# Projection stage of a decoder kernel: four feature steps of a head group issued together, kv sums last, and the last block's queries moved to the last body

## What is computed

```python
qkv = layernorm(x) @ w_qkv                      # 512 -> 3*512
q, k, v = split; 16 heads of 32
q_proj = elu1(einsum('bhnd,hdf->bhnf', q, proj_matrix))   # 128 features a head
k_proj = elu1(einsum('bhnd,hdf->bhnf', k, proj_matrix))
kv    = einsum('bhnf,bhnd->bhfd', k_proj, v)
k_sum = k_proj.sum(axis=2)
# elu1(x) = x + 1 for x > 0, else exp(x)
```

## Time and profile before

| | us |
|---|---|
| median of 3 runs (lowest, highest) | 2795.80 (2794.68, 2798.59) |
| time of the profiled execution | 2796.93 |
| its span, first to last instruction | 2795.2 |
| projection stage within the span | about 0 to 455 |
| PE busy, DVE busy, ACT busy, POOL busy over the span | 2638.4, 1361.0, 858.0, 299.1 |

### The profile page before, as it was taken

One profiled execution on the slowest core, in us unless ns is written; L12 is line 12 of the kernel. 1 busy time (PEld: TensorE's weight loads), 2 busy tenths in 40 slices (PEclk: granted clock), 3 DMA queues, 4 the chain that ended last, 5 costly groups with the idle time before them and its releaser, 6 DMA issues. The chain is left out here.

```text
span 2795.2 us, 34765 instructions
## 1 busy us (share of the span) xinstructions
PE 2638.4 (94%) x12656; PEld 1945.0 (70%) x12680; DVE 1361.0 (49%) x2100; ACT 858.0 (31%) x1364; POOL 299.1 (11%) x228
## 2 busy tenths in 40 slices
PE   7999997899896999799969999999998999999999
PEld 6777774556564554555458888888886888888887
DVE  4544434777765554655463344343335434334433
ACT  3555456455532332133221221111112121112111
POOL 1444343111110111111100000000000000000000
PEclk9999995999997999799989999999999999999999
DMA  6646434554613111212140000000113100000001
GB/s 193 170 98 148 107 87 113 158 156 115 166 75 110 61 54 45 92 61 91 46 155 23 23 23 32 36 23 23 45 45 136 42 26 23 23 23 23 23 23 60
DMA packets 61396, 207.62 MB, mean 74 GB/s; under 512 B 8592, under 2 KB 10384, under 8 KB 50192
## 3 DMA queue, kind: packets, MB, share of 16 engines
q1 hardware_dynamic: 61008, 205.59, 24.4%
q0 software_dynamic: 288, 0.69, 0.1%
HBM read 123.05 MB, written 58.72 MB: 65 GB/s over the span
## 5 line engine op out<-in xcount | busy, mean ns | idle before, releaser
L1876 PE MATMUL ex_pg<-ex_x,ex_w 128*128 128x512 f32 x3840 | 885.5, 390 | 3.3 <-DVE ex_lt L1759 3.3
L1876 PEld LDWEIGHTS ex_pg<-ex_x,ex_w 128*128 128x128 f32 x3840 | 723.3, 188 | 153.7 <-issue 3.5
L1891 PE MATMUL ex_pd<-ex_w,ex_ht 128*128 128x512 f32 x1920 | 446.6, 389 | 0.0
L1825 DVE TENSOR_TENSOR ex_h<-ex_s_g,ex_pg 128x512 f32<-128x512 f32 x160 | 110.1, 688 | 648.6 <-PE ex_pg L1876 647.7
L1891 PEld LDWEIGHTS ex_pd<-ex_w,ex_ht 128*128 128x128 f32 x1920 | 360.5, 188 | 74.7
L1732 ACT ACTIVATE ex_s_g<-ex_pg 128x512 f32<-128x512 f32 x160 | 95.8, 599 | 748.7 <-PE ex_pg L1876 748.6
L1797 DVE SCALAR_TENSOR_TENSOR ex_acc<-ex_pd,ex_share,ex_acc 128x512 f32<-128x512 f32 x320 | 234.4, 748 | 90.3 <-PE ex_pd L1891 84.9
L546 PE MATMUL pr_pj<-pr_xt,pr_w 128*128 128x512 f32 x768 | 194.5, 402 | 4.3 <-DVE pr_xt L443 4.2
L359 POOL TENSOR_TENSOR pr_ks_sum<-pr_ks_sum,pr_kp 128x512 f32<-128x512 f32 x128 | 164.5, 1286 | 228.2 <-DVE pr_kp L490 226.4
L490 DVE SCALAR_TENSOR_TENSOR pr_kp<-pr_pk,pr_kp 128x512 f32<-128x512 f32 x128 | 88.6, 692 | 179.5 <-ACT pr_kp L407 179.1
L546 PEld LDWEIGHTS pr_pj<-pr_xt,pr_w 128*128 128x128 f32 x768 | 142.1, 192 | 33.5 <-issue 2.2
(11 more groups left out here) (175 smaller groups left out, 2856.1 us busy)
## 6 DMA issues: line engine op xcount, KB each, us to landing
stage<-in_units SPq DMA_DIRECT2D x21, 1536.0 KB, 6.6
pr_k<-pr_kq SPq DMA_DIRECT2D x192, 128.0 KB, 2.5
li_q<-q_scratch SPq DMA_DIRECT2D x21, 1024.0 KB, 12.2
q_scratch<-pr_kq SPq DMA_DIRECT2D x128, 128.0 KB, 2.4
x_scratch<-cr_x SPq DMA_DIRECT2D x16, 1024.0 KB, 4.8
pr_x<-in_x SPq DMA_DIRECT2D x8, 1024.0 KB, 6.4
li_x<-in_x SPq DMA_DIRECT2D x8, 1024.0 KB, 5.2
x_scratch<-li_x SPq DMA_DIRECT2D x8, 1024.0 KB, 3.9
```

Of the source, the lines that this page charges most:

```text
L1825: nc.vector.tensor_tensor(h[:, f], s_g[:, f], pg[2 * f + 1][:], ALU.mult).then_inc(h_set, 1)
L1876: mm = nc.tensor.matmul(pg[2 * f + which][:], w[:, slot, sp_, col:col + P], x3[:, m, k, c * TB:(c + 1) * TB], start=(n == 0), stop=(n == 3 ...
L1891: mm = nc.tensor.matmul(pd[t][:], ht[:, s % 2, sp_, f, t * P:(t + 1) * P], w[:, slot, m, WD + f * D:WD + (f + 1) * D], start=(n == 0), sto ...
```

## The change

- PE's loop in a body is no longer by step but by head group g: the four feature steps of the group one behind the other, then a quarter of the body's units, then the four kv sums of this same group. LAG is gone.
- ACT and DVE follow: four steps of exponentials (DVE: four additions), then the reads of all jobs that ended in the group. The statistics of x stand at the end of group 1; the four `norm` stand in group 2, behind the additions and ahead of the reads.
- `kp` has 6 slots for 5, `pk` 4 banks for 3; the kv sums of both batches share one bank (they had one each), and batch 1's first sum waits until DVE has copied batch 0's.
- The four Q jobs of block 7 go from body 6 to body 7; body 6 is left with 8 jobs, body 7 has these 4. Their waits and DMAs move with them.
- SP issues both halves of k and then loads x, where x stood between the halves.

```diff
-    LAG = 2
-    KP_SLOTS, KP_BANKS, BANKS = 5, 3, 3
+    LAST = NBLK - 1
+    KP_SLOTS, KP_BANKS, BANKS = 6, 4, 3
@@ body_jobs
+        if m <= LAST + 1:
+            jobs += [(m if m < LAST else LAST, "Q", g) for g in range(G)] if m != LAST else []
         if m < NBLK:
-            jobs += [(m, "Q", g) for g in range(G)]
@@ plan
-        last = STEPS - 1
-        for s in range(STEPS):
-            part = units[len(units) * s // last:len(units) * (s + 1) // last] if s < last else []
+        for g in range(G):
+            part = units[len(units) * g // G:len(units) * (g + 1) // G]
@@ PSUM
-        p_kv = [... psum_tensor(f"pr_p_kv{b}", [P, 512], F32)) for b in range(NB)]
+        p_kv = ctx.enter_context(nc.psum_tensor("pr_p_kv", [P, 512], F32))
@@ sync
-                        sp.wait_ge(kp_full, STEPS * (m - 1) + (part + 1) * STEPS // PARTS)
+                        sp.wait_ge(kp_full, STEPS * (m - 1) + TT * (2 * part + 2))
...
-                    for part in range(PARTS):
+                    for part in range(PARTS if m < LAST else 0):
                         queries_out(m, part)
                     keys_out(m, 0)
+                    keys_out(m, 1)
...
                         load_x(m + 2)
-                    keys_out(m, 1)
+                for part in range(PARTS):
+                    queries_out(LAST, part)
@@ gpsimd
-                        if n == 6 and i + 2 < NBLK:
+                        if n == 2 * TT - 1 and i + 2 < NBLK:
                             reciprocal_std(i + 2)
@@ scalar
                         if kind == "Q" and m:
-                            act.wait_ge(k3_in[n // 2], 16 * K3_DMAS * m)
-                        if kind == "K":
+                            act.wait_ge(k3_in[n // 2], 16 * K3_DMAS * k_before_q(m))
+                        if kind == "K" and m < LAST:
                             act.wait_ge(q_out[n // 2], 16 * Q_DMAS * (m + 1))
+                        elif kind == "K":
+                            act.wait_ge(k3_in[n // 2], 16 * K3_DMAS * m)
...
-                    for n in range(STEPS):
-                        if i >= 0:
+                    for g in range(G):
+                        for n in range(TT * g, TT * g + TT) if i >= 0 else ():
...
-                        for key in ends(i, n):
+                        for key in ends(i, g):
@@ vector
+                    if i == KV_BODY:
+                        take_kv(0)
+                    for g in range(G):
+                        for n in range(TT * g, TT * g + TT) if i >= 0 else ():
...
+                        if g == 2 and i + 2 < NBLK:
+                            for t in range(TT):
+                                norm(i + 2, t)
+                        for key in ends(i, g):
...
-                        if i == KV_BODY and n == LAG:
-                            take_kv(0)
-                        if i + 2 < NBLK:
-                            if 3 <= n <= 6:
-                                tile_stats(i + 2, n - 3)
-                            if n == 6:
-                                variance(i + 2)
-                            if 8 <= n <= 9:
-                                norm(i + 2, 2 * n - 16)
-                                norm(i + 2, 2 * n - 15)
+                        if g == 1 and i + 2 < NBLK:
+                            for t in range(TT):
+                                tile_stats(i + 2, t)
+                            variance(i + 2)
@@ tensor
+                    if first and i:
+                        pe.wait_ge(kv_taken, i // BLK)
...
-                    for n in range(STEPS):
-                        if i >= 0:
-                            features(i, n)
-                        for key, lo, hi in PLANS[i][n]:
+                    for g in range(G):
+                        for t in range(TT if i >= 0 else 0):
+                            features(i, TT * g + t)
+                        for key, lo, hi in PLANS[i][g]:
                             piece(key, lo, hi)
-                        if i >= 0 and STEPS * i + n >= LAG:
-                            kv(STEPS * i + n - LAG)
-                for step in range(STEPS * NBLK - LAG, STEPS * NBLK):
-                    kv(step)
+                        for t in range(TT if i >= 0 else 0):
+                            kv(i, TT * g + t)
```

More of the change, by code:

```diff
@@ L222, in project, with ends @@
     PLANS = {i: plan(i) for i in range(-1, NBLK)}
-    def ends(i, n):
-        return [key for key, _, hi in PLANS[i][n] if hi == length(key)]
+    def ends(i, g):
+        return [key for key, _, hi in PLANS[i][g] if hi == length(key)]
     JOBS = [(0, "T", t) for t in range(TT)]
@@ L263, in project @@
         pk = [ctx.enter_context(nc.psum_tensor(f"pr_pk{n}", [P, 512], F32)) for n in range(KP_BANKS)]
-        p_kv = [ctx.enter_context(nc.psum_tensor(f"pr_p_kv{b}", [P, 512], F32)) for b in range(NB)]
+        p_kv = ctx.enter_context(nc.psum_tensor("pr_p_kv", [P, 512], F32))
         w_in, x_in = [sem(f"w_in{n}") for n in range(3)], sem("x_in")
@@ L278, in bank_of @@
             return pj[POS[key] % BANKS]
+        k_before_q = lambda m: m if m < LAST else m + 1
         def slot(n):
@@ L381, in take @@
                         if kind == "Q" and m:
+                            act.wait_ge(k3_in[n // 2], 16 * K3_DMAS * k_before_q(m))
+                        if kind == "K" and m < LAST:
+                            act.wait_ge(q_out[n // 2], 16 * Q_DMAS * (m + 1))
+                        elif kind == "K":
                             act.wait_ge(k3_in[n // 2], 16 * K3_DMAS * m)
-                        if kind == "K":
-                            act.wait_ge(q_out[n // 2], 16 * Q_DMAS * (m + 1))
                         nc.scalar.copy(kq[:, HI, n], bank_of(key)[:]).then_inc(act_read, 1)
@@ L452, in take_kv @@
                         dve.wait_ge(filled, POS[(b - 1, "KV")] + 1)
-                    nc.vector.tensor_copy(kv_sum[:], p_kv[b][:]).then_inc(kv_taken, 1)
+                    nc.vector.tensor_copy(kv_sum[:], p_kv[:]).then_inc(kv_taken, 1)
                 def kv_out(b):
@@ L560, in ready @@
                     else:
-                        if kind == "Q" and key[2] == 0:
+                        if kind == ("Q" if m < LAST else "K") and key[2] == 0:
                             pe.wait_ge(dve_read, DVE_AT[(m, "T", TT - 1)])
@@ L579, in features, with kv @@
                     mm.then_inc(kp_full, 1)
-                def kv(step):
-                    i, n = step // STEPS, step % STEPS
+                def kv(i, n):
                     g, t = n // TT, n % TT
+                    step = STEPS * i + n
                     pe.wait_ge(kp_set, step + 1)
@@ L587, in kv @@
                     first, last = i % BLK == 0 and n == 0, i % BLK == BLK - 1 and t == TT - 1
+                    if first and i:
+                        pe.wait_ge(kv_taken, i // BLK)
                     for j in range(HG):
                         h = g * HG + j
-                        mm = nc.tensor.matmul(p_kv[i // BLK][j * HD:(j + 1) * HD, g * F:(g + 1) * F],
+                        mm = nc.tensor.matmul(p_kv[j * HD:(j + 1) * HD, g * F:(g + 1) * F],
                                               v[:, i % 2, t, h * HD:(h + 1) * HD], slot(step)[:, j * F:(j + 1) * F],
```

## The result

| | before | after |
|---|---|---|
| median of 6 runs (us) | 2797.65 | 2777.94 |
| lowest to highest | 2794.68 to 2799.49 | 2765.42 to 2784.84 |
| span of the profiled execution | 2795.2 | 2777.9 |

The ratio is 0.9924, interval 0.9901 to 0.9948: 0.8% faster. The forecast was 2782.5, range 2769 to 2799. The runs spread: over 20 later runs the kernel before went from 2787.66 to 2804.76, so a difference of a few us rests on the profiles and not on the medians.

What follows compares the result with a forecast made beforehand. PE was taken as the bound, with nearly no waiting. Terms +0.5 - 2.5 - 0.8 - 14.6 + 0.6 - 1.5 + 5.0 = -13.3 us took 2796.9 to 2783.6, a median of 2782.5, range 2769 to 2799.

Steps and rivals of the forecast that it cites:

- The largest term: Body 6: loses 48 dense units (11.0 us) to body 7 and gains grouping's 3.6, in all -14.6 us.
- grouping: Per body: four features, then four kv sums in a row save shape changes, -3.6 us before new waits.
- The sums in a row: Kv sums in a group: the first costs 0.56 us, the other three 0.27 each.
- The rival in which each sum waits for the one before: Kv sums 0.42 us apart, 12.6 us given back: 2795, no change; chance 0.07.
- The two new waits: PE in bodies with all jobs: V1 1.7 us late in group 2, V3 1.4 in group 3, together 3.1.
- strict turns: Rival: norms and POOL additions alternate in group 2, norms end at 10.1, six bodies lose 0.9 us each: 2788; chance 0.04.
- The clock: Light work at group boundaries lowers PE's clock: 2 us on bodies 0 to 6, 3 on body 7.
- A body with all jobs: Bodies 0, 1, 2, 3 and 5: down 3.6 us by grouping, up 3.1 by waits, -0.5 each.
- Body 4: With 20 more units: V0 waits 2.2 us and V3 0.6, -0.8 in all; its slow stretch stays.
- Body 7: A chain per group through ACT and DVE, 6.6 us each, to the last sum's start: 26.1 against 25.5, +0.6.
- The end: Kv copy, KV and KS products after body 7: up to 3.4 us gained at full clock, counted as -1.5.
- DMAs: Moved loads and writes of k, x and q cost nothing, unless Q's second half uses up 2 us of slack.

Runs made afterwards that it cites:

- the norms moved: Changed kernel with the four norms of group 2 put behind the reads of that group's jobs (K2, K3): 2761.62 us, ratio 0.9874.
- the transposes last: Changed kernel with the norms behind group 2's reads and group 3 ordered V2, V3, T0, T1, T2, T3: 2758.99 us, ratio 0.9846.
- both orders: Changed kernel with the norms behind group 2's reads and group 3 ordered V2, T0, T1, V3: 2751.31 us, ratio 0.9838.
- body 7 in turn: Norms behind group 2's reads, V2 ahead of T0, and in body 7 alone kv sums alternating with the next group's features: 2752.07 us, ratio 0.9835.
- features and sums in turn: Changed kernel with norms behind group 2's reads, kv sums alternating with the next group's feature steps at every group boundary: 2766.64 us, ratio 0.9889.

## Why the prediction was right, and where its terms were off

- **The gain.** The sum forecast 13.3 us. By the start of the next stage 15.85 are there, over the span 17.3, and the medians differ by 19.7; what lies beyond 15.85 no term of the sum covers. The largest term is right: 14.6 was forecast for body 6, 15.8 measured. The move gave its 11 us (44.74 against 33.85), grouping 4.9 for 3.6.
- **The sums in a row** cost 0.22 each and not 0.27. I had taken the value read from kv's own eight records over the lower bound from the next stage's products, and the lower bound was the true one. That is 12 x 0.05 = 0.6 of the 1.3 us by which body 6 did better. Some 0.4 more lies in the units: groups of 40 and of 24 units last 12.10 and 8.46 (a quarter of body 6), 3.64 / 16 = 0.2275 a unit for my 0.23, over 144 units. The rest is not explained.
- **The rival in which each sum waits for the one before** is refuted: sums follow each other 0.22 apart, while the eight records of one last 0.42. The Trainium skill ("TensorE: Matmul & The Clock Gate", What overlaps and what doesn't) says that a weight load runs beside matmuls in flight only when its row group differs. This trace differs from that: all kv products use the same rows, and the 32 loads of four sums, 105 to 111 ns each, are over after 0.81 us while their products take 1.08, so a sum's loads run beside the products of the one before.
- **The two new waits.** Place, cause and releaser came out as written: V1 behind K2's low part, V3 behind T0's. V3's was 1.47 for 1.4; V1's mostly 2.3 for 1.7, in the range of 0.7 to 2.6 (body 0's, 2.63, just outside). Body 4's were 2.74 for 2.2 and 0.61 for 0.6. The mis-sized term is the norms, 3.5 us for the 3.0 that I took as the middle: POOL's additions ran beside them until 191.10. They ended at 9.7, between free running (8.2) and strict turns (10.1). With the norms moved they take 2.8. The Trainium skill ("SBUF — State Buffer", Who interferes with whom) has an exclusive lock between the two engines; the longer norms agree with that, but no run here isolates it.
- **The clock** is the term that failed. I had named it as a sign of being wrong if PEclk falls in bodies 0 to 3, and it fell in 0, 1 and 3. 2 us were set on bodies 0 to 6. Six short falls came, five behind the V1 waits, at 1.5 each 9 us in all. That the time stayed inside the range is partly luck: the 1.3 us more that grouping saved in each of seven bodies, also some 9 us, was not foreseen either and made up for the falls and the longer waits. That those in bodies 0 to 3 and 5 follow V1's wait, and not the light work alone that I had in mind (features, sums), is shown by moving the norms, which ended them, and by the transposes last, which brought none. In body 7, where waits and light work come together, light work can still matter: see the fall with the norms moved. Behind the same wait the clock falls in one body and not in the next; what decides that stays open.
- **A body with all jobs**: forecast -0.5, measured +0.4 to +1.0 with a fall, -1.1 without. Without one it is -4.9 + 2.3 + 1.5 = -1.1, with the saving as body 6 gave it and the two waits; the falls turned that into a loss.
- **Body 4**: -0.8 forecast, -2.6 measured. I had kept the slow stretch of 9.8 us as it was; it became two short ones.
- **Body 7**: +0.6 forecast and measured, at full clock; the 3 us for the clock were not needed. I had not seen that grouping without the Q units would make it longer (28.43).
- **The end**: -1.5 forecast, nothing measured: from the last sum to the next stage's first product it is 18.31 us, before 18.34. The KS products took 6.96 us (before 6.83), at half clock from near their start. The gain that I had in mind is there in the runs with the norms moved: 5.18 us with both orders, 5.84 with the transposes last, and 3.80, 3.63 and 3.63 with the norms moved alone, body 7 in turn, and features and sums in turn. With them the next stage starts 16.1 to 17.2 us behind the last sum. In the three shortest the last four sums run without a wait right behind the dense units, and KS follows 2.6 us after these; in the changed kernel it is 3.8. But it is 3.8 with both orders too, whose KS took 5.18. So the forecast failed in counting on full clock there because dense units stand before; what decides it is not shown. The norms moved alone:

```profile
409.90 1.08 PE L599 MATMUL pr_p_kv<-pr_kp,pr_v 128*32 128x128 f32 x32
412.06 0.63 PE L541 MATMUL pr_pj<-ident,pr_kv_sum 128*128 128x128 f32 x4 [1.08 <-DVE pr_kv_sum L461]
412.52 3.80 PE L543 MATMUL pr_pj<-pr_ones,pr_ks_sum 128*128 128x2 f32 x32
```

- **DMAs**: nothing, as forecast. The next stage's reads of q are issued 3.25 us after DVE starts its copies of the KS result in the changed kernel (441.94 - 438.69) and 3.26 before. With the norms moved alone, where KS ends sooner, it is 4.5; the last writes of q, issued there until 416.05, may be what is waited for, which is not tested.

## What to carry to other kernels

Batching small matmuls of one shape saves the change of shape for all but the first, but it also batches what ACT and DVE do with them, and every bank's reader then stands behind the batch: list, job by job, which bank is due when, and put optional work of the reading engine (here the norms) behind the reads. An idle PE of some 2 us can cost more than itself, as the clock may fall behind it. Work moved into an underused stage can be nearly free when it fills the time in which PE would wait.

## What was not expected of the hardware

- Eight kv records of 128 columns on 32 columns of the array follow the last eight of the same shape after 0.22 us; with a change of shape to features and back they cost 0.51 to 0.56.
- With PE idle for 2.3 to 2.7 us in an otherwise dense stretch the clock fell to 1.2 GHz in 12 of 18 cases over three profiles, mostly for some 3.4 us, at a cost of 1.5 us. Behind V3's waits of 0.6 to 1.5 us it did not fall in the changed kernel, nor behind the six with the norms moved alone; but that run has a fall in body 7 behind a wait of 0.66 us among sums and features.
